# Two 8-dimension attentions of the last batch from masked 32-row groups, first loads with their own semaphores, and engine orders written out

## The chip, the cores and the metric

The kernel runs on one core of a Trainium2 chip. The metric is device time in microseconds, lower is better. The engines are TensorE (PE; PEld is its weight load), VectorE (DVE), ScalarE (ACT), GpSimd (POOL), and SyncE (SP), which issues most of the DMAs. Each engine takes its instructions strictly in program order and waits on semaphores between engines.

## The reference, cut to what matters

Eight batches of 256 tokens with 128 features pass through two layers, each a cross attention and a mixture of experts; `ctx` has 512 tokens of 96 features per batch.

```python
x = x + tanh(g_xattn[0]) * L0_xattn(layernorm(x), ctx)   # 8 heads of 64, Wq Wk Wv Wo
x = x + tanh(g_ffn[0])   * L0_ffn(layernorm(x))          # self attention, 16 heads of 8, + top-2 of 8 experts
x = x + tanh(g_xattn[1]) * L1_xattn(layernorm(x), ctx)   # cross attention, 16 heads of 8
x = x + tanh(g_ffn[1])   * L1_ffn(layernorm(x))          # top-2 of 8 experts
# each attention: softmax(q k^T / sqrt(d)) v, per batch and head
```

## The kernel before, in words

Work is cut into streams per batch b: **X** (cross attention with 64-wide heads), **F** (self attention with 8-wide heads and the experts), **K** (keys and values of the second cross attention, from `ctx`), **B** (that attention) and **C** (the second experts). A batch goes X, F, B, C, since each reads the residual of the one before; K needs only `ctx`. Different batches overlap: while batch 7 is in F, batch 6 is in B and batch 5 in C. In the last batch less and less is left beside it.

A step of TensorE is a *fill*: some matmuls into one PSUM bank (or two, for wide ones), which then belongs to ScalarE or VectorE until they have drained it. The fills that matter here:

- `ln`: two transposes of the normed rows; the norm is `ls` (VectorE statistics), `rs` (GpSimd, rsqrt by a power) and `xh` (VectorE).
- `kp`, `vp`, `qp`: projections of X. `kk`, `vv`: keys and values of K. `qk`: queries (and in F keys) of the 8-wide attentions.
- `mx`, `mx8`: scores for the maxima. They are made from bfloat16, queries on rows, and VectorE takes the negated maximum over the keys.
- `mT`, `mT8`: those maxima are transposed so that they can be added as one more row of a contraction.
- `e`, `e8`: scores again, keys on rows, with the maxima added by a matmul; ScalarE drains a unit of 128 x 1024 with one exponential.
- `pv`, `pv8`: probabilities times values with a column of ones for the denominators; `oT` transposes them and VectorE divides.

An 8-wide head is a bad fit for a contraction over 128 rows. The kernel before builds *stacks*: ScalarE writes queries and keys in bfloat16 and float32 (L818, L819), GpSimd splits what is left into two more bfloat16 parts (`sp`, L1062 to L1064), SP writes the parts to DRAM (`sw`, L531, L535) and reads them back so that 6 parts x 8 dimensions of a head stand in 48 rows (`sr`, L545, L548); two heads lie in rows 0 to 47 and 64 to 111. The maxima go out and back too (`mw` L571, `mr` L576) as row 49 of the stack. An `e8` unit is then four bfloat16 matmuls of 49 rows and 256 columns, and `pv8` uses four 32-column tiles of TensorE at once.

X has no stacks: an `e` unit (L636, L640) is, for each of two key blocks, two float32 matmuls of 64 rows in the two row halves and then two bfloat16 matmuls that add the maxima row through the tile `pick`.

The order of the work on each engine is made when the program is built: `schedule()` takes each job's planned time and, from `AMOUNTS`, a due time, and always takes the job that can start soonest, with the due time and a cost for a change of tile shape as tie-breakers. It also gives each fill its PSUM banks, and puts *fillers* (L596, matmuls of `wqx` that nobody reads) ahead of a fill for which the plan sees TensorE idle. Each engine's program then walks its list and waits where data or a buffer is not there.

At the start SP issues ten loads (`xin`, `ctx`, and eight that count into one semaphore `w_first`: `ident`, `wkx`, `wqx`, the gates, two biases, `wvx`) and then 19 more that count into `w_loaded`. TensorE, ScalarE and GpSimd wait for the whole of `w_first` before their first work; TensorE also waits until VectorE has cleared all of PSUM (L833). GpSimd first fills the k and v tiles with ones (L1013), then scales the biases, builds `pick`, and only then takes its list, in which the first job is the residual of batch 0 and the second its `rs`.

Of the kernel before, what the change touches and what calls it, by code (L numbers as in the profile page):

```python
# [13 lines left out]
P = 128  # L14
# [13 lines left out]
BANKS = 8  # L28

# [1099 lines left out]
```

## Time and profile before

| | us |
|---|---|
| median of 3 runs (lowest, highest) | 736.36 (733.67, 737.97) |
| the profiled execution | 737.18 |
| its span | 735.3 |
| TensorE busy | 649.0 (88%), 5616 matmuls |
| VectorE busy | 520.3 (71%) |
| ScalarE busy | 401.1 (55%) |
| GpSimd busy | 401.2 (55%) |
| DMA moved | 40.62 MB, mean 55 GB/s |

The span is the time from the first to the last instruction of one profiled execution. Busy time is a mean over a start, a middle and an end with different limits. In the chain that ended last, which the profile follows back from the last instruction, TensorE holds 54%, VectorE 21%, GpSimd and ScalarE 8% each. The largest groups of TensorE are X's score matmuls (L636, 76.9 us), the output products of B (L737, 64.1 us) and of X (L649, 62.1 us); of VectorE, the maxima of B (L992, 148.3 us).

### The profile page before, as it was taken

To read this page: it belongs to the slowest core of one execution; us is meant where nothing else is said; L and a number is where in the kernel's file an instruction comes from. 1 tells how busy PE (TensorE), PEld (TensorE's weight loads), DVE (VectorE), ACT (ScalarE), POOL (GpSimd) and SP (SyncE) were. 2 spreads that over 40 slices of the span, in tenths; PEclk is the share of its full clock that TensorE was granted. 3 is DMA by queue.
4 is the path that set the end of the run, shared out by engine and by line. 5 is a ranking of instruction groups with operands and counts; after the bars stand their busy time and mean duration, and the time that the engine had idled before them with its cause. 6 is when DMAs were issued, how large, how long until landed. Compare 5 with 4: busy or idle time off the path is not lost.

```text
span 735.3 us, 14119 instructions
## 1 busy us (share of the span) xinstructions
PE 649.0 (88%) x5616; PEld 338.8 (46%) x5616; DVE 520.3 (71%) x993; ACT 401.1 (55%) x562; POOL 401.2 (55%) x551
## 2 busy tenths in 40 slices
PE   3998997899899999999999998999999897897882
PEld 1564453554345533554454544554364444343541
DVE  2607557698758787897869787897778658958513
ACT  2463547456845675458655784558543861573350
POOL 7275784771575567628565566636663685040234
PEclk9999999999999999999999999999999999999898
DMA  6130324410060045102350046104420434210000
GB/s 184 40 71 18 75 44 65 98 45 2 9 139 3 12 95 104 44 12 68 78 98 2 20 95 115 28 14 86 89 48 12 89 81 111 44 45 8 2 8 8
DMA packets 64369, 40.62 MB, mean 55 GB/s; under 512 B 5032, under 2 KB 62320, under 8 KB 64304
## 3 DMA queue, kind: packets, MB, share of 16 engines
q1 hardware_dynamic: 64304, 39.72, 25.2%
q8 instruction: 44, 0.72, 0.4%
q14 instruction: 21, 0.17, 0.1%
HBM read 22.80 MB, written 16.91 MB: 54 GB/s over the span
## 4 chain that ended last, share of the span: by engine, by line
PE 54%; DVE 21%; POOL 8%; ACT 8%; issue 5%; DMA 2%; SPq 1%; POOLq 0%; DVEq 0%
PE psum L737 9%; PE psum L649 8%; PE psum L636 7%; DVE mx8B L992 7%; DVE mxA L917 3%; ACT probB L825 3%; PE psum L706 3%; PE psum L609 3%; PE psum L725 3%; PE psum L693 3%; PE psum L614 2%; ACT probX L806 2%; PE psum L700 2%; PE psum L640 2%; PE psum L596 1%
## 5 line engine op out<-in xcount | busy, mean ns | idle before, releaser
L992 DVE TENSOR_REDUCE mx8B<-psum 128x2 f32<-128x1024 f32 x128 | 148.3, 1215 | 13.7 <-PE psum L706 13.2
L825 ACT ACTIVATE probB<-psum 128x1024 f32<-128x1024 f32 x128 | 125.7, 1026 | 18.1 <-PE psum L725 17.6
L917 DVE TENSOR_REDUCE mxA<-psum 128x2 f32<-128x1024 f32 x64 | 76.7, 1217 | 35.2 <-PE psum L620 35.0
L806 ACT ACTIVATE probX<-psum 128x1024 f32<-128x1024 f32 x64 | 65.4, 1026 | 49.0 <-PE psum L640 48.7
L987 DVE TENSOR_REDUCE mx8F<-psum 128x4 f32<-128x1024 f32 x64 | 75.8, 1219 | 11.0 <-PE psum L700 10.0
L636 PE MATMUL psum<-qA,kA 64*128 64x256 f32 x512 | 76.9, 393 | 0.6 <-ACT mrow L779 0.5
L825 ACT ACTIVATE probF<-psum 128x1024 f32<-128x1024 f32 x64 | 63.4, 1023 | 16.9 <-PE psum L725 16.0
L1048 POOL TENSOR_TENSOR sums<-sums,probX 128x512 f32<-128x512 f32 x32 | 40.6, 1270 | 56.8 <-ACT probX L806 55.5
L737 PE MATMUL psum<-probB,v8B 128*9 128x256 f32 x1024 | 64.1, 393 | 4.6 <-ACT probB L825 2.8
L649 PE MATMUL psum<-probX,vX 128*64 128x256 f32 x512 | 62.1, 385 | 2.4 <-ACT probX L806 2.4
L706 PE MATMUL psum<-k8B,q8B 48*128 48x512 bf16 x256 | 47.2, 388 | 12.0 <-DVE mx8B L992 6.9
L1045 POOL TENSOR_TENSOR sums<-probX 128x512 f32<-128x512 f32 x32 | 40.6, 1268 | 19.2 <-ACT probX L806 19.1
L725 PE MATMUL psum<-q8B,k8B 49*128 49x256 bf16 x512 | 47.2, 274 | 3.0 <-ACT probB L825 2.0
L636 PEld LDWEIGHTS psum<-qA,kA 64*128 64x128 f32 x512 | 40.0, 189 | 17.8 <-issue 3.1
L649 PEld LDWEIGHTS psum<-probX,vX 128*64 128x64 f32 x512 | 34.0, 136 | 25.7 <-ACT probX L806 7.0
L1069 POOL TENSOR_TENSOR prodC<-prodC 128x256 f32<-128x256 f32 x32 | 23.3, 727 | 41.2 <-DVE prodC L980 41.0
L609 PE MATMUL psum<-cTX,wkx 96*128 96x512 f32 x64 | 34.5, 665 | 10.9 <-DMA wvx<-in_wvx 10.9
L1049 POOL TENSOR_TENSOR sums<-sums,probX 128x512 f32<-128x512 f32 x32 | 40.7, 1271 | 2.5
L737 PEld LDWEIGHTS psum<-probB,v8B 128*9 128x9 f32 x1024 | 25.6, 92 | 34.8 <-issue 6.1
L725 PEld LDWEIGHTS psum<-q8B,k8B 49*128 49x128 bf16 x512 | 17.5, 94 | 50.4 <-ACT probB L825 16.0
L1053 POOL TENSOR_TENSOR sums<-sums 128x512 f32<-128x512 f32 x16 | 20.3, 1268 | 33.5 <-DVE sums L926 33.5
L737 PE MATMUL psum<-probF,v8F 128*9 128x256 f32 x512 | 33.6, 380 | 3.7 <-ACT probF L825 2.7
(203 smaller groups left out, 1262.3 us busy)
## 6 DMA issues: line engine op xcount, KB each, us to landing
k8B<-k_dK SPq DMA_DIRECT2D x16, 384.0 KB, 6.0
k_dK<-partsK SPq DMA_DIRECT2D x8, 384.0 KB, 2.6
q8F<-q_dF SPq DMA_DIRECT2D x16, 192.0 KB, 4.5
k8F<-k_dF SPq DMA_DIRECT2D x16, 192.0 KB, 5.1
q8B<-q_dB SPq DMA_DIRECT2D x16, 192.0 KB, 3.8
k_dK<-partsK SPq DMA_DIRECT2D x8, 256.0 KB, 2.9
cTX<-in_ctxT SPq DMA_DIRECT2D x8, 192.0 KB, 2.7
cTK<-in_ctxT SPq DMA_DIRECT2D x8, 192.0 KB, 3.1
```

The lines of the kernel that those rows point to most:

```text
L609: last = mm(ps[:, j * KV:(j + 1) * KV], wkx[:, (2 * k + j) * P:(2 * k + j + 1) * P], cT["X"][:], start=True, stop=True)
L636: mm(ps[:, 512 * i + SEQ * c:512 * i + SEQ * (c + 1)], kA[half_i, h, (2 * f + c) * P:(2 * f + c + 1) * P], qA[half_i, h, :], start=True, s ...
L649: last = mm(ps[64 * i:64 * i + 64, 0:SEQ], vX[:, c, h * XD:(h + 1) * XD], prob[s][(2 * k + c // 2) % SLOTS[s]][:, o:o + SEQ], start=(c == ...
L706: last = mm(ps[:, KV * i:KV * (i + 1)], q8[s][b % TURNS[s]][64 * i:64 * i + KROWS, p, t * P:(t + 1) * P], k8[s][b % TURNS[s]][64 * i:64 * ...
L725: last = mm(ps[:, 512 * i + SEQ * c:512 * i + SEQ * (c + 1)], k8[s][b % TURNS[s]][64 * i:64 * i + MROWS, p, (c0 + c) * P:(c0 + c + 1) * P] ...
L737: last = mm(ps[32 * i:32 * i + D8 + 1, 0:SEQ], v8[s][:, c, h, :], prob[s][(NPAIR * KEYS[s] // SEQ * b + u) % SLOTS[s]][:, o:o + SEQ], star ...
L806: nc.scalar.activation(prob[s][k % SLOTS[s]][:], ps, ACT.Exp, scale=float(XD) ** -0.5).then_inc(done["ACT"], 1)
L825: nc.scalar.activation(prob[s][(units * b + k) % SLOTS[s]][:], ps, ACT.Exp, scale=float(D8) ** -0.5).then_inc(done["ACT"], 1)
L917: nc.vector.tensor_reduce(mxA[:, t, h:h + 65:64], ps.rearrange("p (i n) -> p i n", i=2), AX.X, ALU.max, negate=True).then_inc(drained, 1)
L987: nc.vector.tensor_reduce(mx8[s][:, :, 2 * k:2 * k + 2].rearrange("p t i -> p i t"), ps.rearrange("p (i t n) -> p i t n", i=2, t=QT), AX.X ...
L992: nc.vector.tensor_reduce(mx8[s][:, t, 2 * p:2 * p + 2], ps.rearrange("p (i n) -> p i n", i=2), AX.X, ALU.max, negate=True).then_inc(drain ...
L1049: engine.tensor_tensor(sums[:, h], sums[:, h], p[:, :, 1, :], ALU.add).then_inc(S["X"]["psum"], 1)
```

## The change

For the last batch (`LAST = 7`) F and B have no stacks. The head dimension stays in its natural order, so 128 rows hold 16 heads of 8, four to each group of 32 rows. Queries are made four times (j = 0 to 3), each time with all rows but those of head j of each group set to zero by a mask; the keys are used as they are. A product over one 32-row group then gives the scores of one head, and the maxima are added by a product with ones over 32 rows. `tqb` and `tqf` are the two query fills (bfloat16, drained by VectorE; float32, drained by ScalarE), `tkb` F's keys, `tmx` the maxima, `tmT` their transposes (one per j), `te` the scores and `tpv` the products with the values. X's tiles (`qA`, `kA`, `kAb`, `mrow`, `sums`) hold them, and `wqx`, `wkx` get the weights by a late load `tw`. `K` of the last batch writes its keys directly.

Second, the first loads get a semaphore each, four of them are issued by ScalarE, and TensorE waits only for what a fill reads. PSUM is cleared in two pieces, and four matmuls on zeros run between them. GpSimd's fills of the k and v tiles, its biases and `pick` become jobs of its list (`sets`, `bo`, `pick`).

Third, `AMOUNTS` and the greedy choice go; each engine's order is a string of letters, one per job, and `schedule()` only gives banks and fillers along it.

```diff
+LAST = BATCH - 1
+ROWS = 32
+GROUP = P // ROWS
-START = 13.
+START = {"PE": 5.4, "DVE": 5.2, "ACT": 5.0, "POOL": 1.3, "SP": 9.0}
...
+    "POOL": (("X", "rs"), ("X", "pick"), ("X", "bo"), ("K", "sets"), ("X", "xb"), ("X", "e"), ("X", "xs"), ("F", "rs"),
...
+    "POOL": "dabcelaffffffffgghfeiajfffjffffjjkgghelimfnjofajjffjfffkfgghmiejjjofpnjfflkfaffffqgmghqeqqiraopfjffjflffjjkfqfqg"
...
         @block.tensor
-            pe.wait_ge(w_first, W_FIRST)
+            pe.wait_ge(c_set, X_SETS)
             pe.wait_ge(ps_set, 1)
+            for _ in range(EARLY_FILLERS):
+                early = mm(psum[:, 0, 0:SEQ], mxA[:, 0, :], mxA[:].rearrange("p t n -> p (t n)"), start=True, stop=True)
+            early.then_inc(warmed, 1)
+            pe.wait_ge(ps_set, 2)
...
+                elif name in ("tqb", "tqf", "tkb"):
+                    pe.wait_ge(loaded["last"], 32)
+                    pe.wait_ge(*is_done(s, "ln", b))
+                    last = mm(ps[:, 0:SEQ], wkL[s] if name == "tkb" else wqL[s], xT[s][:], start=True, stop=True)
+                elif name == "tmx":
...
+                    for t in tiles:
+                        for g in (2 * i, 2 * i + 1):
+                            o = 512 * (g % 2) + SEQ * t * (s == "F")
+                            last = mm(ps[:, o:o + KEYS[s]], qAb[ROWS * g:ROWS * g + ROWS, j, t * P:(t + 1) * P],
+                                      keyLb[s][ROWS * g:ROWS * g + ROWS], start=True, stop=True, tile_position=(ROWS * g, 0))
+                elif name == "tmT":
+                    pe.wait_ge(t_set, GROUP + 1)
+                    pe.wait_ge(*is_done(s, "tmx", b, (k + 1) * (KEYS[s] // P) - 1))
+                    for t in range(QT):
+                        last = transpose(ps[:, t * P:(t + 1) * P], mxL[k][:, t, :], ident[:])
+                elif name == "te":
...
+                    for c in range(2):
+                        for g in (2 * i, 2 * i + 1):
+                            o, rows = 512 * (g % 2) + SEQ * c, slice(ROWS * g, ROWS * g + ROWS)
+                            mm(ps[:, o:o + SEQ], keyL[s][rows, (c0 + c) * P:(c0 + c + 1) * P], qA[rows, j, :],
+                               start=True, stop=False, tile_position=(ROWS * g, 0))
+                        for g in (2 * i, 2 * i + 1):
+                            o, rows = 512 * (g % 2) + SEQ * c, slice(ROWS * g, ROWS * g + ROWS)
+                            last = mm(ps[:, o:o + SEQ], onesL[rows], rowL[j][rows], start=False, stop=True, tile_position=(ROWS * g, 0))
...
         @block.scalar
-            act.wait_ge(w_first, W_FIRST)
+            engine.dma_start(wkx[:], a["wkx"]).then_inc(loaded["wkx"], 16)
+            engine.dma_start(ident[:], a["ident"]).then_inc(loaded["ident"], 16)
...
+                    for j in range(GROUP):
+                        last = nc.scalar.activation(qA[:, j, :], ps[:, 0:SEQ], ACT.Identity, bias=bqm[s][:, j:j + 1], scale=mask[:, j:j + 1])
...
         @block.vector
+                    for j in range(GROUP):
+                        last = nc.vector.tensor_scalar(qAb[:, j, :], ps[:, 0:SEQ], mask[:, j:j + 1], bqm[s][:, j:j + 1], ALU.mult, ALU.add)
...
         @block.gpsimd
             for s, name, b, k in ORDER["POOL"]:
+                elif name == "sets":
+                    for tile in (*k8["F"], *k8["B"], v8["F"], v8["B"]):
+                        engine.memset(tile[:], 1.0).then_inc(k_set, 1)
+                    pool.wait_ge(w_loaded, W_LOADS)
+                    for to, n in (("F", 0), ("B", 2)):
+                        engine.tensor_scalar(bqm[to][:], mask[:], bqn[:, n:n + 1], None, ALU.mult).then_inc(k_set, 1)
```

In the strings a letter names a step by its place in the list of steps: for GpSimd `a` is X's `rs`, `b` `pick`, `c` `bo`, `d` `sets`, `e` X's `xb`. TensorE's written order begins `kp`, `vp`, `ln`, `kk`, `qp`, `vp`, `vv`, `mx`, `vv`, `mx`, `mx`, `kp`, `mx`, `ln` of batch 1, ... Before it began `kp`, `ln`, `kp`, `qp`, `vp`, `mx`, `mx`, `vp`, `mx`, `mx`, `ln` of batch 1, ... VectorE's written order has `vv` and then, between the maxima of batch 0, the norm of batch 1. In the last batch the `te` units of one j stand among the `tmx` units of the next, and batch 6's `e8` and batch 5's expert fills stand between the end of F and the first `te` of B.

## Rows read from the trace of the kernel before

**Rows 1.** Busy time by stage: stretch, length, busy us (instructions) of each engine, clock, DMA
```profile
35.52:536.04 500.52, 464.93 (x4121) 242.95 (x4121) 373.84 (x693) 299.92 (x420) 302.72 (x399) 1.00 0.28 57
536.04:585.67 49.63, 44.69 (x463) 25.34 (x459) 39.60 (x65) 27.38 (x36) 27.07 (x29) 0.97 0.22 52
585.67:642.29 56.62, 48.47 (x412) 23.63 (x413) 44.63 (x83) 25.67 (x41) 25.08 (x42) 1.00 0.39 78
642.29:690.96 48.67, 41.30 (x314) 22.00 (x313) 32.16 (x70) 18.93 (x27) 12.08 (x24) 0.89 0.08 20
690.96:711.52 20.56, 17.68 (x207) 8.00 (x207) 5.80 (x25) 16.55 (x21) 7.83 (x16) 1.00 0.03 8
711.52:735.30 23.78, 9.33 (x40) 5.76 (x40) 8.63 (x36) 0.98 (x3) 8.63 (x18) 0.85 0.02 6
```

**Rows 2.** The same stretches, fillers of L596 alone: length, busy us of TensorE
```profile
585.67:642.29 56.62, 7.08 (x28) 1.00 0.39 78
642.29:690.96 48.67, 10.79 (x36) 0.89 0.08 20
690.96:711.52 20.56, 1.56 (x6) 1.00 0.03 8
```

**Rows 3.** Timeline of TensorE in the last batch: start us, us, instruction, idle before
```profile
620.82 0.39 PE L711 MATMUL psum<-ident,mx8F 128*16 128x128 f32 x2 [0.21 <-DVE mx8F L987]
...
625.68 0.39 PE L725 MATMUL psum<-q8F,k8F 49*128 49x256 bf16 x4
...
660.75 0.39 PE L706 MATMUL psum<-k8B,q8B 48*128 48x512 bf16 x2
```

**Rows 4.** Timeline of SP's queue: the last B query parts to DRAM
```profile
651.90 1.46 SPq L531 DMA_DIRECT2D q_dB<-partsB  x3
```

**Rows 5.** Timeline of TensorE: X's score units of batch 0
```profile
36.14 0.63 PE L636 MATMUL psum<-qA,kA 64*128 64x256 f32 x4
...
36.68 0.63 PE L636 MATMUL psum<-qA,kA 64*128 64x256 f32 x4
...
37.23 0.63 PE L636 MATMUL psum<-qA,kA 64*128 64x256 f32 x4
```

**Rows 6.** Timeline of TensorE: B's score units and output product of batch 6
```profile
649.73 0.83 PE L725 MATMUL psum<-q8B,k8B 49*128 49x256 bf16 x12
...
652.81 0.39 PE L725 MATMUL psum<-q8B,k8B 49*128 49x256 bf16 x4
653.14 1.91 PE L737 MATMUL psum<-probB,v8B 128*9 128x256 f32 x32
```

**Rows 7.** Timeline of ScalarE: four exponentials in a row
```profile
650.84 3.75 ACT L825 ACTIVATE probB<-psum 128x1024 f32<-128x1024 f32 x4
```

**Rows 8.** Line L671, F's query fill: duration ns min/median/max, first and last start
```profile
L671 PE MATMUL psum<-xTF,wq8F x16: 379/431/483, 75.0 to 590.9; 128*128 128x256 f32 x16
```

**Rows 9.** Timeline of TensorE: first projection, transpose, maxima; a later projection
```profile
10.90 3.78 PE L609 MATMUL psum<-cTX,wkx 96*128 96x512 f32 x4 [10.90 <-DMA wvx<-in_wvx]
15.99 0.69 PE L601 MATMUL psum<-ident,xhX 128*128 128x128 f32 x2 [1.30 <-DVE xhX L902]
...
24.75 0.61 PE L620 MATMUL psum<-kAb,qAb 64*128 64x512 bf16 x4 [0.31 <-ACT qA L791]
...
45.50 1.98 PE L609 MATMUL psum<-cTX,wkx 96*128 96x512 f32 x4
```

**Rows 10.** Timeline of GpSimd: the last fill and the first rsqrt
```profile
9.98 0.59 POOL L1013 MEMSET v8B<- 128x576 f32 x1
...
14.26 0.23 POOL L1027 TENSOR_SCALAR veX<-mvX 128x2 f32<-128x2 f32 x1
```

**Rows 11.** Timeline of SP's queue: the last weights are issued
```profile
14.02 0.43 SPq L556 DMA_DIRECT2D weB<-in_weB  x1
```

**Rows 12.** Busy time by stretch around the last weights: last column GB/s moved
```profile
16.00:17.00 1.00, 1.00 (x3) 0.81 (x4) 0.00 (x0) 0.94 (x2) 0.00 (x0) 1.00 1.06 311
17.00:18.00 1.00, 1.00 (x2) 0.34 (x1) 0.00 (x0) 0.10 (x1) 0.00 (x0) 1.00 1.11 368
```

More of the change, by code:

```diff
@@ L138, in plan_x @@
         g = UNITS * b + k - SLOTS["X"]
-        p.fill("ACT", 1, "X", "e", b, k, 1.08, .91, [("ACT", "X", "mT", b, 0)],
+        p.fill("ACT", 1, "X", "e", b, k, 1.08, .91, [("ACT", "X", "mT", b, 0), ("POOL", "X", "pick", b, 0)],
                [("PE", "X", "pv", g // UNITS, g % UNITS // 2), ("POOL", "X", "e", g // UNITS, g % UNITS)])
@@ new lines, in plan_direct @@
+def plan_direct(p, s, b, keys, v, old):
+    n = KEYS[s] // P
+    units = GROUP * n
+    for k in range(units):
+        p.fill("DVE", 1, s, "tmx", b, k, .22, 1.13, [("DVE", s, "tqb", b, 0), keys], [("POOL", "F", "tset", b, 0)])
+        if k % n == n - 1:
+            p.fill("ACT", 0, s, "tmT", b, k // n, .22, .3, [("DVE", s, "tmx", b, k)], [("POOL", "F", "tset", b, 0)])
+    for k in range(units):
+        g = units * b + k - SLOTS[s]
+        old_pv = ("PE", s, "tpv", b, (k - SLOTS[s]) // n) if k >= SLOTS[s] else ("PE", s, "pv8", b - 1, 3)
+        p.fill("ACT", 1, s, "te", b, k, 1.08, .91, [("ACT", s, "tmT", b, k // n), ("ACT", s, "tqf", b, 0)], [old_pv])
+    for k in range(GROUP):
+        p.fill("ACT", 0, s, "tpv", b, k, .435 * n, .3, [("ACT", s, "te", b, n * (k + 1) - 1), v], [("PE", s, "oT", b - 1, 1)])
+    for k in range(QT):
+        p.fill("DVE", 0, s, "oT", b, k, .44, .9 if s == "F" else .5, [("ACT", s, "tpv", b, 3)], old)
@@ L209, in plan_k @@
     for k in range(2):
-        p.fill("DVE", 0, "K", "vv", b, k, .45, .33, [("SP", "K", "ctx", b, 0)], [("PE", "B", "pv8", b - 1, 3)])
+        p.fill("DVE", 0, "K", "vv", b, k, .45, .33, [("SP", "K", "ctx", b, 0)], [("PE", "B", "pv8", b - 1, 3), ("POOL", "K", "sets", b, 0)])
 def plan_b(p, b):
@@ L231, in slack, with turns @@
 def slack(key):
+    if key in (("SP", "X", "xin", 0, 0), ("SP", "X", "ctx", 0, 0)):
+        return 0.
     return OUT if key[0] == "PE" else LAND[key[1:3]] if key[0] == "SP" else 0.
-def targets(jobs):
-    count = {}
-    for e, s, name, b, k in jobs:
-        count[e, s, name] = max(count.get((e, s, name), 0), k)
-    out = {}
-    for key in jobs:
-        group, b, k = key[:3], key[3], key[4]
-        off, step = AMOUNTS[group]
-        out[key] = PERIOD * b + off + step * (k / count[group] if count[group] else 0.)
-    return out
+def turns(p):
+    groups, order = {}, {}
+    for key in p.jobs:
+        groups.setdefault(key[:3], []).append(key)
+    for e, letters in TURN_OF.items():
+        steps = [groups.pop((e, *group)) for group in STEPS[e]]
+        left = [iter(keys) for keys in steps]
+        order[e] = [next(left[LETTERS.index(letter)]) for letter in letters]
+        assert len(order[e]) == sum(len(keys) for keys in steps)
+    assert not groups
+    return order
 def free_banks(wide, bank_free, now):
@@ L261, in schedule @@
     jobs = {key: (busy, [a for a in after if a in p.jobs]) for key, (busy, after) in p.jobs.items()}
-    later = {key: [] for key in jobs}
-    for key, (_, after) in jobs.items():
-        for a in after:
-            later[a].append(key)
-    wanted = targets(jobs)
-    left = {key: len(after) for key, (_, after) in jobs.items()}
-    at = dict.fromkeys(jobs, 0.)
-    free = {"PE": START, "DVE": 0., "ACT": START, "POOL": 0., "SP": 0.}
-    could = {e: [key for key in jobs if key[0] == e and left[key] == 0] for e in free}
+    turn = turns(p)
+    free, at = dict(START), dict.fromkeys(turn, 0)
     never = 1e9
@@ L322, in schedule, with ready @@
-    return order, bank_of, before, p.drain, over, warm
+    over, before, warm = {}, {}, {}
+    def ready(key):
+        e, after = key[0], jobs[key][1]
+        if any(a not in over for a in after):
+            return None
+        return max([over[a] + HOP * (a[0] != e) for a in after], default=0.)
+    while len(over) < len(jobs):
+        went = False
+        for e in ("SP", "POOL", "ACT", "DVE"):
+            while at[e] < len(turn[e]) and ready(turn[e][at[e]]) is not None:
+                key = turn[e][at[e]]
+                free[e] = max(free[e], ready(key)) + jobs[key][0]
+                over[key] = free[e] + slack(key)
+                at[e] += 1
+                went = True
+                if p.drain.get(key[1:]) == e:
+                    for i in range(BANKS):
+                        if held[i] == key[1:]:
+                            bank_free[i] = over[key] + HOP
+        if went:
+            continue
+        key = turn["PE"][at["PE"]]
+        fill, other = key[1:], MODE.get(key[1:3], 0) != mode
+        start = max(free["PE"] + DRAIN_OUT * other, ready(key))
+        when, banks = free_banks(p.wide[fill], bank_free, start)
+        assert when < never
+        start = max(start, when)
+        idle = start - max(free["PE"], when)
+        warm[fill] = int(min(20, max(0., idle - IDLE) // WARM_UP)) if WARM else 0
+        before[fill] = [held[i] for i in banks if held[i]]
+        bank_of[fill] = banks[0]
+        for i in banks:
+            held[i], bank_free[i] = fill, never
+        free["PE"] = start + jobs[key][0]
+        if other:
+            mode = MODE.get(key[1:3], 0)
+            free["PE"] += ENTRY.get(key[1:3], .1)
+        over[key] = free["PE"] + slack(key)
+        at["PE"] += 1
@@ L325 @@
+    return {e: [key[1:] for key in keys] for e, keys in turn.items()}, bank_of, before, p.drain, over, warm
 ORDER, BANK, FORMER, DRAIN, OVER, WARMERS = schedule()
@@ L387, in build @@
         wo8 = sb("wo8", [P, P])
+        bqn = sb("bqn", [P, 4])
+        mask = sb("mask", [P, GROUP])
+        bqm = {s: sb("bqm" + s, [P, GROUP]) for s in "FB"}
         wg = {s: sb("wg" + s, [P, NE]) for s in "FB"}
@@ L422, in build @@
         prodX = [sums[:, 2 * n:2 * n + 2].rearrange("p h i n -> p (h i n)") for n in range(QT)]
+        mxL = [sums[:, j, 0, :].rearrange("p (t n) -> p t n", t=QT) for j in range(GROUP)]
+        rowL = [kAb[:, 2 + j // 2, SEQ * (j % 2):SEQ * (j % 2) + SEQ] for j in range(GROUP)]
+        keyL = {"F": kA[:, 0, 0:SEQ], "B": kA[:, 1, :]}
+        keyLb = {"F": kAb[:, 0, 0:SEQ], "B": kAb[:, 1, :]}
+        onesL = mrow[:, 0:P]
+        wqL = {"F": wqx[:, 0:P], "B": wqx[:, 2 * P:3 * P]}
+        wkL = {"F": wqx[:, P:2 * P], "B": wkx[:, 0:P]}
         width = {"F": 2 * SEQ, "B": SEQ, "K": KV}
@@ L563, in _ @@
                     load_ctx(s, b)
+                elif name == "tw":
+                    sp.wait_ge(*is_full("X", "qp", b))
+                    sp.wait_ge(*is_full("X", "kp", b, 1))
+                    engine.dma_start(wqx[:, 0:3 * P], a["wqL"]).then_inc(loaded["last"], 16)
+                    engine.dma_start(wkx[:, 0:P], a["wkL"]).then_inc(loaded["last"], 16)
                 elif name == "sw":
```

332 lines of the change are left out of this document (216 added, 116 removed), and 53 rows, old and new, of tables (AMOUNTS, STEPS).

## The prediction, as made before the result was known

> **What bounds the kernel now.** I read the busy time by stage first. The stretches [rows 1] are cut at four events of the last batch: the first score unit of its cross attention X (536.04), the transpose that opens its stage F (585.67), the last output transpose of F (642.29), and the score units and the end of B (690.96, 711.52). The reader is to see that TensorE is the bound in the long middle, 464.9 of 500.5 us (93%), with VectorE at 75%; that no engine bounds the three stretches from 585.67 to 711.52; and that the last 23.78 us are a chain of short steps. In the stretch from 536.04 to 711.52 (49.63 + 56.62 + 48.67 + 20.56 = 175.5 us) TensorE shows 44.69 + 48.47 + 41.30 + 17.68 = 152.1 us, but 7.08 + 10.79 + 1.56 = 19.4 of them are fillers that compute nothing [rows 2]. Own work is 132.7 us, 76%, so some 43 us are waits. The second reading, the timelines, tells which: F's maxima are transposed at 620.82, go through DRAM, and its score units start at 625.68 [rows 3]; the last B query parts leave at 651.90 [rows 4] and the first maxima unit of that B starts at 660.75 [rows 3]. The profiled execution took 737.18 us for its span of 735.3, against a median of 736.36; sums below are made from 737.2, and 0.8 is taken off at the end.
>
> **Part 1, the last batch without stacks: what goes.** The trips through DRAM go: 9 us for the B queries, some 5 us for each set of maxima, and GpSimd's splits with them. They are the waits of the 43 us, not work of TensorE. Late behind them is TensorE itself.
>
> **What comes on TensorE.** A score unit becomes two float32 matmuls and two bfloat16 ones per half, in 32 rows. The trace has no 32-row pair; the nearest is X's score unit, the same eight matmuls in pairs of 64 rows: a half takes 36.14 to 36.68, two of them 36.14 to 37.23, so 1.09 us a unit [rows 5]. A score unit of before costs 0.22: three of them (twelve matmuls) last 0.83, one 0.39, so (0.83 - 0.39) / 2 [rows 6]. There are 8 units in F and 16 in B: 24 x (1.09 - 0.22) = 20.9 us. The ends: if a pair of 32 rows runs one after the other, a unit is 2.18 and the term 47; if units overlap better, ScalarE's exponentials, four in 3.75 us or 0.94 each [rows 7], keep the term at 17 in a stream of units. I take 20.9, by the nearest row. The maxima units keep their number (8 and 16) and their VectorE work.
>
> Queries and keys: five fills (two for F's queries, one for its keys, two for B's queries) in place of three. Two more of two records at 0.43 [rows 8] are at most 1.7; pipelined about half of that, so 1.0. Eight transposes of maxima in place of two: 6 x 0.22 = 1.3.
>
> The written order has more changes of tile shape: counted in the two orders, 486 against 421 in all, 137 against 105 behind the first X score unit of the last batch. The row: a pair of 32-column tiles follows a 48-row unit after 0.33 us (652.81 to 653.14) where a further such unit follows after 0.22 [rows 6], so 0.11 a change: 32 x 0.11 = 3.5 us in the tail, 33 x 0.11 = 3.6 ahead of it. The Trainium skill, "TensorEngine Tiling (Array Packing)", section "Tiling Modes", says that changing the tiling mode, and not just the tile, drains the engine; the trace agrees with 0.11 us. Without that rule the sum would be 7.1 us lower.
>
> Moved: by the written order eight fills that stood ahead of that X unit come behind it, and one goes the other way. By their kinds (two value fills of the size of the later key projection 1.98 [rows 9], one B output product 1.91 [rows 6], two expert products and small ones) they are worth 8.4 us. This is neutral but for where it lies.
>
> **The tail summed.** 132.7 own work, less some 3 us for stretches where the clock granted fell (0.89 from 642.29 to 690.96 [rows 1]; a denser engine idles less), + 20.9 + 1.0 + 1.3 + 3.5 + 8.4 = 164.8 us of TensorE work. How long that takes depends on the waits left. At the middle's density of 93% it is 177 us, at 100% 165. The new order lets one head group's scores start while the next group's maxima run, and batch 6's B scores and outputs and batch 5's expert products stand between the end of F and the first B score unit of batch 7: an estimated 22 us of TensorE work (16 score units 3.5, four output products 7.6, three expert products 3, eight maxima units 1.8, the rest fills and changes) against a chain of some 16 us (division and norm 6, queries 2, four maxima units with expert drains between them 7, transpose 1). So I take 96%: 171.7 us against 175.5, that is -3.8. VectorE (122 of 175.5 before) gets 3 us more, ScalarE (88.5) the same; both hide.
>
> **The middle.** The 8.4 us moved out and one 1.1 us fill that now lies in the head, less 3.6 for changes, at 93%: -5.9 / 0.93 = -6.3. The new order itself I cost at nothing, since the idle left there is only 36 us in 500; bounds -12 to +6. The end chain is unchanged in its steps.
>
> **Part 2, the first loads: what goes and what comes.** TensorE no longer waits for eight loads (its first projection started at 10.90 [rows 9]); it can start at about 5.5, when the PSUM clear ends. But GpSimd's written order opens with the step that fills the k and v tiles, ahead of the first norm's rsqrt, and that step now ends with a wait for all weights. Before, the fills ended at 10.57 and the rsqrt of batch 0 started at 14.26 [rows 10]. The last weights were issued at 14.02 [rows 11]; the queue then moved 311 and 368 GB/s until about 18 [rows 12], of which 0.52 MB are theirs and come first, so they were in at about 17.6. With four loads moved to ScalarE and two new small ones SP issues them two slots, 0.95 us, earlier: in at 16.7, rsqrt at about 17.2, 2.9 us later than before. Queued behind that wait on GpSimd are the rsqrt, the pick tile, the biases and the residual; for the rsqrt wait VectorE's scaling, TensorE's transpose (1.73 us behind it, 14.26 to 15.99), the queries and all maxima.
>
> From the transpose to the first maxima unit passed 8.76 us (15.99 to 24.75 [rows 9]), with 3.6 us of key projection in it. That now lies in the early gap, but in its place comes the key fill of B, half as long, which TensorE does after a long wait: four records of such a size took 3.78 us after the first wait and 1.98 later [rows 9], so its two take 1.7 to 1.9. So 18.9 + 8.8 - 3.6 + 1.7 = 25.8, 1.0 late; then VectorE has the second batch's norm between the maxima (1.3). The first score unit, at 35.52 before, is late by about 2.3; I take +2.5 (the 1.1 us fill done by then is credited in the middle). Bounds: -1 (TensorE at its later speed, VectorE hidden) and +4 (the early speed for all of it).
>
> **Sum.** 737.2 - 3.8 - 6.3 + 2.5 = 729.6; against the median, 728.8. I say 728.5, its own range 721 to 735.
>
> **Rivals.**
> (a) The waits come back. For it: every engine runs in a written order, so one late step stalls it, and the head is late against any plan. Against it: the joint of F and B in the last batch has 6 us to spare. At the middle's density the tail takes 177 us (+1.5), and if the new order gains only half of the middle's term (-3): 737.2 + 1.5 - 3 + 2.5 - 0.8 = 737.4. Chance 0.18.
> (b) Slower: 32-row pairs do not run side by side. Place: the 24 score units, of which B's stand on the path. Price 24 x 1.09 = 26 us more, 24 of them bare: 752.5. It decides from an extra 0.33 us a unit (7.9 / 24). For it: no row shows this shape. Against it: 48-row pairs do. Chance 0.09.
> (c) Four tiles of 32 rows run at a time, so that neighbouring units overlap and ScalarE paces them: TensorE's unit falls below the 0.94 of an exponential [rows 7]; 24 x (1.09 - 0.94) = 3.6 us: 725. Chance 0.08. The Trainium skill names up to 4x for a contracted size of 32 or less ("TensorEngine Tiling (Array Packing)", "Theoretical Speedup"); no run here shows it, and the pairs are issued two at a time.
> (d) The separate semaphores do what they say, and the rsqrt starts when the fills end (10.6 in place of 14.26): -3.7 in place of +2.5, 722. Against it: the wait stands in GpSimd's order. Chance 0.05.
> (e) The written order takes a third of the middle's 36 us of idle: -12, 716.5. For it: VectorE, ScalarE and GpSimd all have room there. Against it: 93% is near full. Chance 0.13.
>
> **How the numbers follow.** The forecast has 0.47. Within 0.5% of the median (732.7 to 740), which is about what a measurement can tell from no change, lie 0.06 of the forecast and 0.10 of (a): 0.16. Faster: 0.41 of the forecast, (c), (d), (e): 0.67. Slower: (b) and 0.08 of (a): 0.17. The range 714 to 743 leaves out (b), the ends of (e) and of (a).
>
> **What would show it.** Right: the batch 0 rsqrt at 16.5 to 18 behind the weights; first X score unit at 36.5 to 39; score units of the last batch 1.0 to 1.2 us apart; hardly any fillers and TensorE above 90% from 585 to 705; the last 23 to 24 us as before. Wrong: units at 2 us, a rsqrt at 11, or TensorE idle again between F and B of the last batch.

## The result, and the profile after

The changed kernel takes 744.66 us in the median of 6 runs (742.35 to 747.85), the kernel before on the same chip 737.9: a ratio of 1.0106, 95% interval 1.0071 to 1.0141. It is slower, where 728.5 was forecast and 714 to 743 was the range. The profiled execution took 747.85 us with a span of 746.1, 10.8 us more than the 735.3 of before.

Busy time by stage, cut at the same events as [rows 1] (the last stretches are cut at the end of F's output transposes, the first direct B score unit and the first of B's last output transposes):

```profile
39.34:549.43 510.09, 473.42 (x4070) 242.84 (x4070) 365.67 (x688) 293.43 (x416) 288.00 (x374) 0.97 0.23 50
549.43:607.90 58.47, 54.72 (x533) 29.59 (x533) 46.30 (x88) 31.66 (x44) 40.92 (x56) 1.00 0.45 88
607.90:658.50 50.60, 47.70 (x435) 24.18 (x436) 43.51 (x72) 26.27 (x43) 19.63 (x40) 0.98 0.09 24
658.50:683.86 25.36, 24.34 (x229) 9.45 (x228) 17.64 (x47) 19.92 (x29) 8.72 (x18) 0.91 0.02 6
683.86:722.28 38.42, 36.69 (x383) 21.49 (x381) 21.04 (x48) 19.30 (x27) 7.05 (x13) 1.00 0.00 1
722.28:746.10 23.82, 9.33 (x40) 5.76 (x40) 8.64 (x36) 0.98 (x3) 10.97 (x25) 0.83 0.04 11
```

The differences from [rows 1]: the head +3.8 (39.34 against 35.52), the middle +9.6 (510.09 against 500.52), the tail -2.6 (58.47 + 50.60 + 25.36 + 38.42 = 172.85 against 175.48), the end chain 23.82 against 23.78. The sum is +10.8. Head and tail are near the forecast (+2.5 and -3.8). The middle was to give 6.3 and cost 9.6.

The reader should look at two columns of the middle's row. TensorE's idle time is 510.09 - 473.42 = 36.7 us, and it was 500.52 - 464.93 = 35.6: the same. What grew is the busy time, for less work (4070 matmul records against 4121), and the granted clock went from 1.00 to 0.97. The same view in short stretches shows where (columns as above):

```profile
116.00:124.00 8.00, 6.04 (x66) 1.75 (x64) 7.47 (x11) 6.61 (x9) 6.56 (x11) 1.00 0.07 25
124.00:128.00 4.00, 2.50 (x24) 1.08 (x28) 2.00 (x2) 2.08 (x3) 2.46 (x3) 0.88 0.73 150
128.00:136.00 8.00, 8.00 (x46) 3.82 (x39) 3.07 (x6) 3.46 (x8) 2.01 (x3) 0.63 0.31 42
184.00:192.00 8.00, 5.39 (x50) 2.61 (x48) 6.75 (x9) 3.24 (x4) 5.77 (x8) 0.99 0.59 101
192.00:204.00 12.00, 11.53 (x84) 5.22 (x84) 5.36 (x19) 7.96 (x10) 1.87 (x4) 0.58 0.01 1
312.00:318.00 6.00, 2.47 (x28) 1.48 (x25) 1.92 (x5) 2.56 (x5) 4.39 (x6) 1.00 1.01 152
318.00:326.00 8.00, 7.50 (x50) 3.65 (x46) 6.21 (x17) 3.07 (x3) 5.54 (x6) 0.79 0.18 51
326.00:332.00 6.00, 2.62 (x8) 0.79 (x8) 5.88 (x8) 0.00 (x0) 5.56 (x7) 0.70 0.00 0
332.00:340.00 8.00, 8.00 (x47) 3.90 (x45) 6.54 (x7) 0.38 (x1) 2.50 (x4) 0.80 0.00 0
```

Each stretch in which TensorE is thin (6.04 of 8, 5.39 of 8, 2.47 of 6, 2.62 of 6) is followed by one in which it is nearly full and runs in part at the lower of its two levels, 1.2 in place of 2.4 GHz. Clock missing (one minus the clock) times length adds up in these rows to 0.5 + 3.0 + 0.1 + 5.0 + 1.7 + 1.8 + 1.6 = 13.7 us, and a last fall, 0.79 from 372 to 380, adds 1.7. The timeline of TensorE names the five waits of over 1 us in the middle (last bracket: idle us before, and who ended it):

```profile
124.83 0.44 PE L676 MATMUL psum<-ident,xhF 128*128 128x128 f32 x2 [1.52 <-DVE xhF L1057]
144.37 0.44 PE L676 MATMUL psum<-ident,xhB 128*128 128x128 f32 x2 [1.75 <-DVE xhB L1057]
192.16 0.61 PE L850 MATMUL psum<-q8B,k8B 49*128 49x256 bf16 x4 [2.04 <-DMA q8B<-m_dB]
317.22 0.39 PE L825 MATMUL psum<-k8F,q8F 48*128 48x256 bf16 x4 [3.53 <-DMA k8F<-k_dF]
329.38 2.08 PE L818 MATMUL psum<-weB,xTC 128*128 128x512 f32 x2 [3.88 <-DVE prodC L1164]
```

In the kernel before the same view has ten such waits in the middle, none over 1.5 us. The longest:

```profile
131.71 0.38 PE L715 MATMUL psum<-ident,wF 128*8 128x128 f32 x2 [1.47 <-DVE wF L875]
```

In the changed kernel a wait's length alone does not decide: behind the 1.75 us at 144.37 the clock stayed at 1.00 (136 to 152), and ahead of the fall near 372 no wait is over 1 us.

### The profile page after: what moved, and what is told of

It reads as the page before. It is cut to its first block, busy times and chain, and to the rows that moved or that the text cites. A ratio compares the mean times of both kernels' runs of the same rounds, so it can differ in the third digit from the quotient of the medians.

```text
span 746.1 us, 14417 instructions
## 1 busy us (share of the span) xinstructions
PE 676.4 (91%) x5776; PEld 350.7 (47%) x5776; DVE 519.3 (70%) x1000; ACT 402.8 (54%) x574; POOL 393.6 (53%) x549
## 4 chain that ended last, share of the span: by engine, by line
PE 53%; DVE 23%; issue 7%; ACT 7%; POOL 4%; DMA 2%; SPq 1%; POOLq 0%; DVEq 0%; ACTq 0%
PE psum L862 7%; PE psum L714 6%; PE psum L727 6%; DVE mx8B L1176 5%; PE psum L818 5%; DVE mxA L1072 3%; PE psum L850 3%; PE psum L686 3%; DVE mx8F L1171 3%; PE psum L831 2%; ACT probB L980 2%; PE psum L692 2%; PE psum L681 2%; PE psum L867 2%; DMA k8F<-k_dF 1%
## 5 line engine op out<-in xcount | busy, mean ns | idle before, releaser
L1176 DVE TENSOR_REDUCE mx8B<-psum 128x2 f32<-128x1024 f32 x112 | 132.1, 1216 | 12.6 <-PE psum L831 11.6
L980 ACT ACTIVATE probB<-psum 128x1024 f32<-128x1024 f32 x112 | 109.4, 1030 | 27.3 <-PE psum L850 22.0
L714 PE MATMUL psum<-qA,kA 64*128 64x256 f32 x512 | 77.2, 394 | 1.6 <-ACT mrow L910 0.9
L1171 DVE TENSOR_REDUCE mx8F<-psum 128x4 f32<-128x1024 f32 x56 | 66.5, 1217 | 11.0 <-PE psum L825 10.6
L980 ACT ACTIVATE probF<-psum 128x1024 f32<-128x1024 f32 x56 | 56.7, 1026 | 21.3 <-PE psum L850 20.4
L862 PE MATMUL psum<-probB,v8B 128*9 128x256 f32 x896 | 55.3, 388 | 1.6 <-DVE mx8F L1171 0.8
L714 PEld LDWEIGHTS psum<-qA,kA 64*128 64x128 f32 x512 | 40.2, 189 | 23.2 <-issue 5.5
L831 PE MATMUL psum<-k8B,q8B 48*128 48x512 bf16 x224 | 40.9, 385 | 3.2 <-DVE mx8B L1176 0.8
L818 PE MATMUL psum<-weB,xTC 128*128 128x512 f32 x64 | 36.2, 656 | 3.9 <-DVE prodC L1164 3.9
L1164 DVE TENSOR_TENSOR prodF<-psum,wF 128x512 f32<-128x512 f32 x32 | 21.6, 684 | 23.9 <-PE psum L818 22.8
L718 PE MATMUL psum<-mrow,pick 64*128 64x256 bf16 x256 | 35.8, 272 | 0.0
L818 PE MATMUL psum<-weF,xTF 128*128 128x512 f32 x64 | 34.8, 628 | 0.8 <-DVE mxA L1072 0.7
```

What stands on the lines that cost most here:

```text
L714: mm(ps[:, 512 * i + SEQ * c:512 * i + SEQ * (c + 1)], kA[half_i, h, (2 * f + c) * P:(2 * f + c + 1) * P], qA[half_i, h, :], start=True, s ...
L818: last = mm(ps, xT[s][:, t * P:(t + 1) * P], we[s][:, f * 512:(f + 1) * 512], start=True, stop=True)
L831: last = mm(ps[:, KV * i:KV * (i + 1)], q8[s][b % TURNS[s]][64 * i:64 * i + KROWS, p, t * P:(t + 1) * P], k8[s][b % TURNS[s]][64 * i:64 * ...
L862: last = mm(ps[32 * i:32 * i + D8 + 1, 0:SEQ], v8[s][:, c, h, :], prob[s][(NPAIR * KEYS[s] // SEQ * b + u) % SLOTS[s]][:, o:o + SEQ], star ...
L980: nc.scalar.activation(prob[s][(units * b + k) % SLOTS[s]][:], ps, ACT.Exp, scale=float(D8) ** -0.5).then_inc(done["ACT"], 1)
L1171: nc.vector.tensor_reduce(mx8[s][:, :, 2 * k:2 * k + 2].rearrange("p t i -> p i t"), ps.rearrange("p (i t n) -> p i t n", i=2, t=QT), AX.X ...
```

## The experiments

Theory O is that the written order of batches 0 to 6 costs the time; its mechanism, theory C, that it gathers the idle into heaps, behind which TensorE works for a while at half its clock. Rival N is that the new last batch or the loads cost it, rival S that the stalls alone do. Ratios are against the kernel before on the same chip. Fillers ahead of a step are those that the plan gives for the order in question, unless said otherwise.

**The order undone.** On each engine the order of the kernel before up to the first X score unit of the last batch, the written one behind it. SP's line stands for the five:

```diff
-    "SP": "abgagbhbacdefbaicdjkehflimcadjgkebflhmacgnibdjkefhlmacdibjknegflhmicdajgknbeflmchdojikgefhnlmijknglmnnn",
+    "SP": "bagabhgibacdhefiacbdjkeflmacdbjkefglmahincdbjkefglmahincdbjkefglmahincdbjkefglmhincdojkgefhlmijknglmnnn",
```

> The changed kernel, with the orders of the kernel before on all engines up to the first X score unit of the last batch (GpSimd still opens with the step that waits for all weights), and the written order behind it. Theory O (the written order of batches 0 to 6 costs the time: the middle took 510.1 us where the forecast had 494): the middle falls back to about 500, the eight moved fills are done in the middle again, so the end is 8.7 us shorter; against the 744.7 median of the changed kernel that is -9.6 - 8.7 = 726, range 723 to 732; granted clock in the middle 0.99 or more. Rival N (the new last batch, its steps and loads or the longer program cost it, wherever the orders come from): 741 to 748. Rival W (the lost time is only moved: what the middle regains the end gives back in waits): 735 to 741.

726.75 us, ratio 0.9873 (0.9828 to 0.9919). Middle and tail of its profile:

```profile
39.17:538.88 499.71, 466.12 (x4125) 243.15 (x4125) 373.85 (x693) 299.75 (x421) 302.65 (x400) 1.00 0.26 58
538.88:702.03 163.15, 151.81 (x1523) 78.54 (x1522) 125.56 (x248) 93.41 (x135) 62.45 (x101) 1.00 0.10 25
```

The middle is that of the kernel before (499.71), the tail is 163.15, where 172.85 - 8.7 = 164.2 was expected. Theory O holds, rivals N and W fall. The old orders repeat: in SP's line `mahincdbjkefgl` stands three times in a row. The written one has no such period.

**The last batch undone.** The written order kept, the stacks of the last batch back, in the order of the kernel before:

```diff
-LAST = BATCH - 1
+LAST = BATCH
```

> The changed kernel with its head and its written order up to the first X score unit of the last batch, but the last batch with stacks again, in the order of the kernel before from there on. Theory O: the middle is as slow as in the changed kernel (about 510 us, clock 0.97), and the end is that of the kernel before, 175.5 us, plus the 8.7 us of moved work in place of 172.9: 744.7 + 11.3 = 756, range 750 to 760. Rival N (the new last batch costs the time, the order nothing): 737.9 and the late head, 3.8: 738 to 743.

773.12 us, ratio 1.0517 (1.0462 to 1.0571), outside both ranges. Rival N falls again. (That the new last batch is a gain, the run before shows: 163.15 us of tail in place of 175.48, with the same work ahead of it.) The middle is as expected, the end is not: from the first X score unit of the last batch on it takes 217.27 us in place of 175.5 + 8.7 + 23.8 = 208, at a clock of 0.90. Clock missing times length is 21.7 us there, against 1.5 + 5.4 + 3.6 = 10.4 us in the same stretches of [rows 1], so falls of the clock can account for the 9 us; why they come at this seam between the two orders was not followed up.

```profile
40.83:553.93 513.10, 476.71 (x4123) 244.83 (x4123) 368.49 (x690) 296.44 (x421) 294.78 (x388) 0.98 0.23 51
553.93:771.20 217.27, 172.60 (x1440) 90.39 (x1436) 132.54 (x281) 89.56 (x127) 86.98 (x141) 0.90 0.20 45
```

**Where in the order.** The old order only up to the transpose of F of batch 4:

```diff
-    "SP": "abgagbhbacdefbaicdjkehflimcadjgkebflhmacgnibdjkefhlmacdibjknegflhmicdajgknbeflmchdojikgefhnlmijknglmnnn",
+    "SP": "bagabhgibacdhefiacbdjkeflmacdbjkefglmahincdbjkefglmahcdibjknegflhmicdajgknbeflmchdojikgefhnlmijknglmnnn",
```

> As the first of these kernels, but with the orders of the kernel before only up to the transpose that opens F of batch 4 (353.9 us in the kernel before, 371.6 in the changed one); the written order from there on. Theory L (the written order loses its time between batches 1 and 3, where the clock granted fell, and nothing later: the events of the two kernels stand 0.8 us apart at F of batch 1, 16.6 at F of batch 3 and 15.8 at F of batch 5): 744.7 - 13 = 731, range 727 to 735. Rival E (the written order loses evenly, and a fresh start of it loses again): 737 to 742. Rival N, as above: 741 to 748.

729.99 us, ratio 0.9922 (0.9896 to 0.9948): theory L. Its middle is the most telling row of the study:

```profile
39.03:533.80 494.77, 460.33 (x4076) 240.11 (x4076) 366.72 (x689) 295.13 (x415) 288.72 (x374) 0.99 0.24 53
```

It does the work of the changed kernel's middle (4076 records and 4070) in 494.77 us, where the forecast had 500.5 - 6.3 = 494.2. Against it the changed kernel's 510.09 is 15.3 us more: 13.1 of TensorE's busy time (473.42 against 460.33) and 2.2 of its idle time (36.7 against 34.4). In this middle the clock falls twice (0.86 from 180 to 192 and again from 360 to 372), 3.4 us of clock missing against the changed kernel's 13.7 + 1.7 = 15.4: 12 us of difference, nearly all of the busy time. The second half of the written order is sound (179.21 us from the transpose of F of batch 4 to the end of the middle, 178.11 here); batches 0 to 3 of it cost some 15 us.

**One wait's cause.** SP's queue in the changed kernel before the 3.53 us wait:

```profile
302.80 0.43 SPq L649 DMA_DIRECT2D out<-accC  x1
303.27 1.27 SPq L610 DMA_DIRECT2D k8B<-k_dK  x2
304.58 0.60 SPq L585 DMA_DIRECT2D cTX<-in_ctxT  x1
305.23 0.54 SPq L607 DMA_DIRECT2D q8F<-q_dF  x1
```

The first three stood in the written order ahead of F's stacks of batch 3. The edit puts them behind (`gnibd` becomes `gdibn`: n is the output, i the K stacks, b the context, d the F stacks):

```diff
-    "SP": "abgagbhbacdefbaicdjkehflimcadjgkebflhmacgnibdjkefhlmacdibjknegflhmicdajgknbeflmchdojikgefhnlmijknglmnnn",
+    "SP": "abgagbhbacdefbaicdjkehflimcadjgkebflhmacgdibnjkefhlmacdibjknegflhmicdajgknbeflmchdojikgefhnlmijknglmnnn",
```

> The changed kernel with one move in SP's order: the loads of the F stacks of batch 3 come ahead of the loads of the K stacks of batch 2, of a context and of the first output, behind which they stood. Theory Q (these queue entries held up the stacks: they were issued at 305.2 and landed after 317, and TensorE waited 3.5 us for them): the wait goes below 1 us, the fall of the clock behind it goes too, 3 to 5 us less: 740 to 742. Rival (GpSimd's splits or the next wait, 3.9 us for the expert products at 329, take its place): within 1.5 us of 744.7.

740.11 us, ratio 1.0069 (1.0048 to 1.0089). The stacks are issued at 301.50 (SP's queue), and TensorE has no wait over 1 us from there to 322.82, where the wait for the expert products is 2.81 (its timeline):

```profile
301.50 0.61 SPq L607 DMA_DIRECT2D q8F<-q_dF  x1
```

```profile
322.82 2.08 PE L818 MATMUL psum<-weB,xTC 128*128 128x512 f32 x2 [2.81 <-DVE prodC L1164]
```

From F's transpose of batch 3 to that of batch 4 the trace goes from 81.09 us (289.13 to 370.22) to 76.46 (287.56 to 364.02), 4.6 less, as theory Q had it. The medians alone, from two chips, would not show it.

**The clock.** Fillers in three places where TensorE waited for an operand:

```diff
+WARMERS["F", "ln", 1, 0], WARMERS["B", "e8", 0, 0], WARMERS["F", "mx8", 3, 0] = 3, 4, 7
```

> The changed kernel with its written order, and filler matmuls (they compute nothing) in three places where TensorE waited for an operand: 3 ahead of the transpose of F of batch 1 (1.52 us of wait), 4 ahead of the first B score unit of batch 0 (2.04), 7 ahead of the first F maxima unit of batch 3 (3.53). Theory C (the written order's idle is no larger than before, 36.7 us in the middle against 35.6, but it stands in heaps, and behind each heap TensorE is granted half its clock for some 7 us): behind these three places the granted clock stays at 1.00, which gives back up to 3.4 + 5.1 + 1.7 = 10.2 us; taken 6 to 10, so 735 to 739 against 744.7. Rival S (the stalls themselves cost the time and the clock only follows): a filler saves nothing, 743 to 747.

740.58 us, ratio 1.008 (1.0047 to 1.0112). The median lies between the two ranges, and the interval overlaps the changed kernel's, so both were run again on one chip:

> The changed kernel once more, unaltered, on the chip of the next three, to compare them with. Expected 1.007 to 1.014 of the kernel before, as measured (1.0106). Its profile tells whether the five falls of the granted clock in the middle come in every execution: if the heaps of idle cause them, the ones behind the waits of over 2 us (near 192, 317 and 329) are there again, those behind shorter ones (near 127 and 372) may not be.

746.44 us, ratio 1.0133 (1.0111 to 1.0155). The falls near 127, 192, 317 and 329 are there again, the one near 372 is not.

> The changed kernel with fillers in three places, as before (3, 4 and 7 of them), now on the same chip as the unaltered one. Theory C (behind each heap of idle TensorE works at half the clock; the fillers keep the clock up): 0.5 to 1.1% (4 to 8 us) less than the unaltered kernel. Rival S (the fillers only fill the stalls): within 0.3% of it.

740.09 us, ratio 1.0062 (1.0041 to 1.0083), beside the unaltered kernel 1.0062 / 1.0133 = 0.993: 0.7%, and from the two intervals 0.4 to 1.0%. The same stretches with fillers (behind the second place the program now runs 6 to 8 us earlier):

```profile
124.00:128.00 4.00, 3.33 (x36) 1.36 (x34) 1.90 (x2) 2.07 (x4) 2.36 (x3) 1.00 0.74 149
128.00:136.00 8.00, 8.00 (x62) 4.90 (x60) 6.10 (x20) 3.78 (x10) 2.92 (x3) 1.00 0.36 64
184.00:192.00 8.00, 6.37 (x58) 3.46 (x56) 5.78 (x12) 5.25 (x7) 5.41 (x9) 1.00 0.53 75
192.00:204.00 12.00, 10.65 (x123) 5.16 (x124) 7.63 (x26) 11.33 (x19) 4.38 (x6) 1.00 0.00 0
312.00:318.00 6.00, 5.96 (x50) 2.85 (x46) 5.69 (x16) 3.07 (x3) 4.29 (x5) 1.00 0.27 66
318.00:326.00 8.00, 4.29 (x16) 1.55 (x16) 7.88 (x11) 0.00 (x0) 7.46 (x10) 0.73 0.00 0
```

The clock is 1.00 at the three places. From the first B score unit of batch 0 to F's transpose of batch 2 the same work takes 6.43 us, where it took 9.40 in the changed kernel. Those two stretches (the changed kernel first), and the whole middle with fillers:

```profile
192.16:201.56 9.40, 9.13 (x69) 3.90 (x69) 3.97 (x17) 5.71 (x6) 1.87 (x4) 0.50 0.01 2
189.56:195.99 6.43, 5.39 (x69) 2.49 (x69) 3.21 (x15) 5.61 (x6) 1.87 (x4) 1.00 0.01 3
39.27:541.49 502.22, 470.21 (x4099) 244.12 (x4099) 366.01 (x688) 292.94 (x416) 287.48 (x374) 0.99 0.23 51
```

In that middle TensorE is busy for 470.21 us, 7.54 of them in fillers, so 462.7 with its own work; the unaltered kernel, with 0.70 of fillers, has 472.7. A filler brings no operand earlier; it only keeps TensorE at work. So rival S falls and theory C holds. Of the up to 10.2 us that were expected back, the total shows 5 to 6 (0.7%; the medians are 6.4 apart). The fall at 322 stays: there TensorE waits for a bank that VectorE has not drained, and a filler has no bank to write to. The Trainium skill, "TensorE: Matmul & The Clock Gate", section "HAM oscillation — how this bites in real kernels", describes a kernel whose matmuls run at the lower clock behind each wait for data; the trace agrees, with a clock of 0.58 from 192 to 204 behind the wait for `q8B`, though that kernel's waits are put at 3 to 5 us and this one is 2.04.

**The head.** GpSimd's order opens with `rs`, `pick`, `bo`, `xb` and only then `sets`:

```diff
-    "POOL": "dabcelaffffffffgghfeiajfffjffffjjkgghelimfnjofajjffjfffkfgghmiejjjofpnjfflkfaffffqgmghqeqqiraopfjffjflffjjkfqfqg"
+    "POOL": "abcedlaffffffffgghfeiajfffjffffjjkgghelimfnjofajjffjfffkfgghmiejjjofpnjfflkfaffffqgmghqeqqiraopfjffjflffjjkfqfqg"
```

> The changed kernel with one change in GpSimd's order: the first rsqrt, the pick tile, the biases and the residual come ahead of the step that fills the k and v tiles and waits for all weights. Theory H (the late rsqrt delays the head by itself, and the delay passes through): the rsqrt starts at about 6 in place of 18.2, then TensorE is the limit, whose first projections run from 14.6 to 18.2, so the first transpose starts at 18.3 in place of 20.7 and the first X score unit at 36.5 to 37.5 in place of 39.3; total -2.5, about 742. Rival (the head's delay is hidden by waits further on, or the late fills of the k and v tiles make a new one at the first stacks): within 1 us of 744.7, or above it.

739.86 us, ratio 1.0068 (1.0041 to 1.0095), some 3 to 5 us below the changed kernel's two ratios. The rsqrt starts at 6.03, the first X score unit at 35.25 in place of 39.34: theory H, with 4.1 us in the trace where 2.5 was expected. Not all of the total is the head's: the middle, too, is shorter in this profile (506.39 us against 510.09), with the falls of the clock partly at other places. With the old order for batches 0 to 6, and VectorE's norm of batch 1 (`ab`) behind four maxima (`c`), each line the first of its string:

```diff
-    "DVE": "ababccccccccppccdceecccccfgabhiiikkjkklmmmmmmmmdnceeccccfcgcabhiiikkcokkoqrljmmmmmmmmnsssssssssssssssstdcoeecccc"
+    "DVE": "abccccabccccppccdceecccccfgabhiiikkjkklmmmmmmmmdnceeccccfcgcabhiiikkcokkoqrljmmmmmmmmnsssssssssssssssstdcoeecccc"
```

> The orders of the kernel before up to the first X score unit of the last batch, the new last batch behind it, and the head mended: GpSimd takes the first rsqrt, the pick tile, the biases and the residual ahead of the step that waits for all weights, VectorE the second batch's norm behind the first four maxima. Theory: both repairs add up. The rsqrt repair gave 2.8 us on the changed kernel (first X score unit at 35.3 in place of 39.3): 726.7 less 3 to 4 on the same footing, 0.982 to 0.984 of the kernel before. Rival (the old order has a wait of its own at the first stacks, and the head's gain is lost there): 0.987 as without it.

727.96 us, ratio 0.9901 (0.987 to 0.9931), where 0.982 to 0.984 was expected: a miss, and no gain that can be told from the 0.9873 on another chip, though the first X score unit starts at 36.10 in place of 39.17. The step is inconclusive. Its first projection still stood behind fillers that waited for a weight. Without those:

```diff
+WARMERS["X", "kp", 0, 0] = 0
```

> As the kernel before this one in the list, but without the 7 filler steps that stand ahead of the first projection and wait for a weight that landed at 8.7. Theory F (they hold up the first projection, 14.6 in place of about 6 to 8, and with the rsqrt early nothing else does): the first projection starts at 6 to 8, the first X score unit at 27 to 31, and the total is 4 to 8 us less than with them. Rival G (TensorE then waits for the first transposes at a lower granted clock, or the K stacks, which wait for all weights, are the next limit): within 2 us of the run with them.

723.06 us, ratio 0.9838 (0.9789 to 0.9887), on the chip of the run with them: 4.9 us less. The first projection starts at 5.19, the first X score unit at 30.26. Theory F. Then the norm of batch 1 behind all eight maxima, and no fillers ahead of the first transpose of the maxima either:

```diff
-    "DVE": "abccccabccccppccdceecccccfgabhiiikkjkklmmmmmmmmdnceeccccfcgcabhiiikkcokkoqrljmmmmmmmmnsssssssssssssssstdcoeecccc"
+    "DVE": "abccccccccabppccdceecccccfgabhiiikkjkklmmmmmmmmdnceeccccfcgcabhiiikkcokkoqrljmmmmmmmmnsssssssssssssssstdcoeecccc"
+WARMERS["X", "kp", 0, 0] = WARMERS["X", "mT", 0, 0] = 0
```

> The orders of the kernel before for batches 0 to 6, the new last batch, the rsqrt early, no fillers ahead of the first projection or of the first transpose of the maxima, and the norm of batch 1 (VectorE's statistics and scaling, TensorE's transpose) behind all eight maxima units of batch 0 in place of four. Theory: VectorE's eight maxima of 1.2 us run in one row from about 15, the first X score unit starts at 26 to 27 in place of 30.3, and as in the step before (5.8 us earlier gave 4.9) most of it passes through: 3 to 4 us less, 0.978 to 0.981 of the kernel before. Rival (the norm of batch 1 is late now and its queries stop TensorE, or the K stacks are the limit): 0.983 to 0.987.

721.14 us, ratio 0.9808 (0.9784 to 0.9833). The first X score unit starts at 25.82. The ratio is inside the forecast (0.978 to 0.981), but a gain over the step before is not shown: the two intervals overlap, and the chips differ. 4.4 us of earliness in the trace go with 0.003 in the ratio, some 2 us. This version beats both kernels (735.96 and 746.44 on its chip).

**The written order repaired.** The early rsqrt and SP's move together, with

```diff
+WARMERS["F", "ln", 1, 0], WARMERS["B", "ln", 0, 0], WARMERS["B", "e8", 0, 0] = 3, 4, 5
```

> The changed kernel in its written order with three repairs together: the early rsqrt, the reads of the F stacks of batch 3 ahead of the three queue entries, and fillers where the profile still shows waits of 1.5 to 2.7 us (3, 4 and 5, ahead of F's transpose of batch 1, of B's transpose and of the first B score unit of batch 0). If each removes a loss of its own (2.8, some 4, some 4 us): 0.992 to 0.999 of the kernel before. Rival (they share one loss, or the wait for the expert products at 329 takes the rest): 1.003 to 1.007. Either way some of the 16 us that the order costs stays, since that last wait is untouched.

732.3 us, ratio 0.9951 (0.9931 to 0.9972), on the chip where the unaltered kernel has 1.0133. The repairs add: 13 to 14 us for three edits that touch no arithmetic. In its middle (35.76 to 535.30, 499.54 us) the clock is 1.00, and TensorE is busy for 468.46 us, 6.68 of them in fillers: 461.8 with its own work, 10.9 less than in the unaltered kernel. So the clock was most of the order's loss and not all of it: 499.54 is still 4.8 us above the 494.77 of the half-old order. What this version lacks against the old order (0.9873, with the late rsqrt) was not taken apart further.

## Why the prediction was wrong

**The step that failed** is the one in the part on the middle: "The new order itself I cost at nothing, since the idle left there is only 36 us in 500; bounds -12 to +6." It cost 15.3 us at equal work (510.09 against 494.77), beyond the bound. The reason given was a true number and the wrong one: the idle hardly changed (36.7 us). It was gathered into four heaps, and behind each TensorE needed more time for the same work: 12 us more of clock missing, of the 15.3. A bound from the sum of the idle cannot see that; the row that could was the clock, 1.00 in [rows 1] for the middle, under an order whose ten waits of over 1 us each stayed below 1.5. The prediction took 3 us off the tail for the clock ("a denser engine idles less"), but in the middle it left the clock as it was. It changes with the order.

**The rest of the middle** was right: the moved work without the order's loss gives 494.77 (forecast 494.2). Only this sum is shown, and in part it may be luck: the 3.6 us in it for changes of tile shape were not measured by themselves, and the kernel of that row has the written order in its second half alone.

**The tail** came to -2.6 where -3.8 was forecast. Its TensorE work was put at 164.8 us, and the rows show 54.72 + 47.70 + 24.34 + 36.69 = 163.5. The density was put at 96% and is 94.6%; one fall of the clock (0.91 from 658.50) is part of that: in the second profile of the unaltered kernel it is not there, and from the first X score unit of the last batch to the end pass 194.37 us in place of 196.67. A score unit of 32 rows was taken from X's unit, 1.09 us [rows 5], and halves of B's units start 0.54 to 0.55 apart, so 1.09 a unit:

```profile
716.83 0.63 PE L787 MATMUL psum<-qA,kA 32*128 32x256 f32 x4
...
717.37 0.63 PE L787 MATMUL psum<-qA,kA 32*128 32x256 f32 x4
...
717.92 0.63 PE L787 MATMUL psum<-qA,kA 32*128 32x256 f32 x4
```

So rivals (b), pairs one after the other, and (c), more of them at once, are out. No filler runs in the tail up to 722.28, as said.

**The head** was +2.5 and came to +3.8. The mechanism is the one named, and its rows answer to [rows 9] and [rows 10]:

```profile
17.65 0.30 POOL L1213 TENSOR_SCALAR bqmF<-mask,bqn 128x4 f32<-128x4 f32 x1 [7.08 <-DMA weB<-in_weB]
...
18.20 0.23 POOL L1224 TENSOR_SCALAR veX<-mvX 128x2 f32<-128x2 f32 x1
```

The weights were in at 17.65 (forecast 16.7), and two small operations stand behind the wait ahead of the rsqrt (18.20, forecast 17.2): 1.0 of the 1.3 us by which the head is later than forecast. The step before it was missed: TensorE was to start its first projection at about 5.5, and started at 14.59, behind 7 filler matmuls that wait for a weight (a float32 matmul leaves two records, so 14 in the row):

```profile
8.68 6.08 PE L670 MATMUL psum<-wox,ident 128*128 128x256 f32 x14 [3.39 <-DMA wox<-in_wox]
14.59 1.88 PE L686 MATMUL psum<-cTX,wkx 96*128 96x512 f32 x4
```

With the rsqrt at 18.2 that cost nothing; with the rsqrt early it was worth 4.9 us.

**The rivals.** (a) named the right thing, a written order in which one late step stalls an engine, but priced it as 1.5 us more in the tail and half of the middle's gain lost, and put 737.4 on it. (d) was out because the wait stands in GpSimd's order, as argued, and (e) had the sign of the order wrong.

## What to carry to other kernels

Two orders with nearly the same idle sum (36.7 and 34.4 us) differed by 15 us: look at how the idle of the bounding engine lies and at the granted clock behind its waits, and price a wait with the slow stretch behind it. A written order that is to replace one which settled into a period needs its waits read batch by batch, the in-order queues first; whether the period itself is what helped is not shown. Where a wait can't go, a few matmuls that compute nothing may pay, if they wait for nothing themselves and a bank is free.

## What the hardware showed

- The clock fell behind a wait of 2.04 us at the end of a thin stretch (5.39 of 8 us busy): it was 0.58 from 192 to 204, with TensorE busy for 11.53 of the 12 us. The same 1.52 us wait at about 125 was followed by a fall in both profiles of the unaltered kernel and by none with SP's move (1.00 from 120 to 136), whose fall near 190 remained.
- A float32 matmul of 32 rows takes as long as one of 64: 374 ns in the median of 192 records (L787), 376 in that of 512 (L714).
- The same issue can hold a queue for longer: three writes of the B query parts took 4.94 us of SP's queue at 307.84, right behind nine other issues, with 163 GB/s moving, where three such writes took 1.43 at 220.76, behind a pause, with 147 GB/s moving. What makes the difference was not looked for.
